# Eleven far taps on SyncE instead of eight, addressed in bytes, in a deformable convolution behind a diffusion stage

## The reference

```
x = x + L0(group_norm(x))     # gates by depthwise 3x3 convolutions, Sobel gradients, 5 diffusion steps
x = x + L1(group_norm(x))     # deformable 3x3 convolution

L1: wi = conv3x3(x, w_offset) + b_offset          # 27 values per pixel: 9 dy, 9 dx, 9 masks
    py, px = base position of the tap + offset    # for each pixel and each of 9 taps
    v00, v01, v10, v11 = the 4 pixels around (py, px), 64 channels each, zero outside the image
    sampled = (bilinear mix of the four) * sigmoid(mask)
    out = sum over taps and channels of sampled * filt
```

## Time and profile before

| | before |
|---|---|
| median of 3 runs | 807.94 us (807.9 to 808.3) |
| the profiled execution, its own time | 803.14 us |
| its span, first to last instruction | 801.3 us |
| granted TensorE clock, mean | 0.904 |
| PE busy | 669.2 us (84%) |
| DVE busy | 539.4 us (67%) |
| POOL busy | 544.0 us (68%) |
| ACT busy | 242.2 us (30%) |
| gathers on POOL | 568 |
| far DMAs on SP | 1024 |

### The profile page before, as it was taken

How to read it: one execution, slowest core, us unless ns; L and a number is a source line. 1 busy time by engine, 2 the same in 40 slices (tenths; PEclk the granted TensorE clock), 3 DMA queues, 4 the chain that set the end, 5 groups by cost and what they waited for, 6 DMA issues and landing times.

```text
span 801.3 us, 15341 instructions
## 1 busy us (share of the span) xinstructions
PE 669.2 (84%) x4616; PEld 589.9 (74%) x4616; DVE 539.4 (67%) x906; ACT 242.2 (30%) x469; POOL 544.0 (68%) x583
## 2 busy tenths in 40 slices
PE   8976888899899988989799987999799987655656
PEld 6865667788788888768689887778778877544545
DVE  5695479778977896578866895778866796322122
ACT  4414421542145213522144313522154213000000
POOL 2000777777777777777777777777777777777774
PEclk9997988999999999999989998999899998555557
DMA  5102333533353433543353435343353335333432
GB/s 167 56 3 55 97 110 109 159 108 115 109 166 109 128 110 112 163 122 109 109 167 114 121 110 167 107 126 108 113 162 114 109 108 167 111 109 108 114 111 72
DMA packets 55146, 92.80 MB, mean 116 GB/s; under 512 B 13384, under 2 KB 35480, under 8 KB 55064
## 3 DMA queue, kind: packets, MB, share of 16 engines
q0 software_dynamic: 27264, 74.49, 31.9%
q1 hardware_dynamic: 27608, 17.20, 7.7%
q10 hardware_dynamic: 192, 0.15, 0.1%
HBM read 79.37 MB, written 12.40 MB: 115 GB/s over the span
## 4 chain that ended last, share of the span: by engine, by line
POOL 57%; issue 20%; PE 12%; DVE 7%; ACT 2%; DMA 1%; POOLq 0%; SPq 0%; DVEq 0%; ACTq 0%
POOL pixels L558 57%; PE banks L1150 9%; PE banks L1153 4%; DVE weighted L903 1%; DMA pixels<-table,index 1%; DVE banks L759 1%; DVE prod L778 0%; DVE prod L798 0%; DVE row_squares L582 0%; ACT coef_T L1051 0%; DVE prod L816 0%; DVE prod L779 0%; ACT sampled_T L1063 0%; DVE banks L760 0%; DMA taps<-taps_in 0%
## 5 line engine op out<-in xcount | busy, mean ns | idle before, releaser
L558 POOL DMA_INDIRECT pixels<-table,index x568 | 538.7, 948 | 247.6 <-issue 172.4
L1153 PE MATMUL banks<-const,weighted 128*128 128x128 f32 x1280 | 194.5, 308 | 62.8 <-DVE weighted L903 49.5
L903 DVE TENSOR_TENSOR weighted<-pixels,banks 128x2304 f32<-128x2304 f32 (+1 forms) x65 | 161.2, 2480 | 115.7 <-DMA pixels<-table,index 111.8
L1153 PEld LDWEIGHTS banks<-const,weighted 128*128 128x128 f32 x1280 | 169.6, 163 | 73.9 <-DVE weighted L903 53.8
L1063 ACT ACTIVATE sampled_T<-banks 128x512 f32<-128x512 f32 (+1 forms) x128 | 55.7, 435 | 335.1 <-PE banks L1153 334.3
L1153 PE MATMUL banks<-const,prod 128*128 128x128 f32 x816 | 109.9, 278 | 19.3 <-DVE prod L778 12.9
L1153 PEld LDWEIGHTS banks<-const,prod 128*128 128x128 f32 x816 | 90.7, 143 | 28.2 <-DVE banks L760 14.1
L1150 PE MATMUL banks<-conv_w,xT 128*128 128x64 f32 (+2 forms) x576 | 97.7, 325 | 0.7 <-ACT banks L1040 0.7
L1150 PEld LDWEIGHTS banks<-conv_w,xT 128*128 128x128 f32 x576 | 91.4, 191 | 7.0 <-ACT banks L1040 1.6
L1150 PE MATMUL banks<-filt,sampled_T 128*128 128x64 f32 x640 | 87.0, 286 | 7.2 <-ACT sampled_T L1063 7.2
L1150 PEld LDWEIGHTS banks<-filt,sampled_T 128*128 128x128 f32 x640 | 81.5, 202 | 13.5 <-ACT sampled_T L1063 11.5
(11 more groups left out here) (144 smaller groups left out, 651.6 us busy)
## 6 DMA issues: line engine op xcount, KB each, us to landing
far_pixels<-table SPq DMA_DIRECT2D x1024, 1.0 KB
pixels<-table,index POOLq DMA_INDIRECT x568, 2.7
table<-xn SPq DMA_DIRECT2D x48, 128.0 KB
table<-xn SPq DMA_DIRECT2D x16, 144.0 KB
x<-x_in SPq DMA_DIRECT2D x30, 64.0 KB, 2.6
out_dram<-x SPq DMA_DIRECT2D x60, 32.0 KB
table<-corner_w SPq DMA_DIRECT2D x16, 70.0 KB
const<-const_in SPq DMA_DIRECT2D x2, 384.0 KB, 3.9
```

What stands on the lines that cost most here:

```text
L558: pool.indirect_dma_start(out=pixels[:, col % NB, k, :], out_offset=None, in_=table[0:(u + 1) * TY * TX, :], in_offset=bass.IndirectOffset ...
L903: return dve.tensor_tensor(weighted[:, col % 2, :, a:b, :].rearrange("p q k c -> p k q c"), entries.rearrange("p k (q c) -> p k q c", c=C) ...
L1153: return pe.matmul(dst, data, moved, start=start, stop=stop, is_transpose=True, skip_group_check=True)
```

## The change

SP fetches the last two taps of the last column of images 2, 4 and 6, and one tap of the others: 11 taps in all instead of 8 (`FAR_TAPS`). POOL gathers three taps fewer. `far_pixels` and the indices (now `far_at`) hold up to two taps. DVE computes the byte address at once (offset added, then times 1024), PE turns one or two columns of indices in its one matmul, and SP reads the table as a flat array of bytes, so that a loaded register is the address as it stands. The fetches of an image are numbered tap by tap: 0 to 127 the first far tap, 128 to 255 the second; the first 32 still come before the output store, and all the rest after it. For the last column of an image with two far taps, DVE's far instruction covers two taps and the other one seven.

```diff
-LAST_TAPS = ((0, 6), (6, 8), (8, K2))
-
-FAR_W, FAR_K = WS - 1, K2 - 1
-FAR_REGS, FAR_FIRST = 16, 32
+LAST_TAPS = ((0, 6), (6, 8))
+
+FAR_TAPS = (1, 1, 2, 1, 2, 1, 2, 1)
+FAR_W, FAR_MOST = WS - 1, max(FAR_TAPS)
+FAR_LOADED, FAR_FIRST = 16, 32
...
-        far_pixels = sb("far_pixels", [P, 2, ENTRY])
-        far_index = sb("far_index", [1, 2, P], u32)
+        far_pixels = sb("far_pixels", [P, 2, FAR_MOST, ENTRY])
+        far_at = sb("far_at", [FAR_MOST, 2, P], u32)
...
+        table_bytes = table.flatten().bitcast(u8)
...
-                for p in range(first, last, FAR_REGS):
-                    sp.load(regs, far_index[0:1, u % 2, p:p + FAR_REGS])
-                    for i in range(FAR_REGS):
-                        sp.dma_start(far_pixels[p + i:p + i + 1, u % 2, :], table[bass.ds(sp.snap(regs[i]), 1), :])\
-                          .then_inc(s_far[u], 16)
+                for n in range(first, last, FAR_LOADED):
+                    tap, p = divmod(n, P)
+                    _, at = nc.values_load_multi_w_load_instructions(
+                        far_at[tap:tap + 1, u % 2, p:p + FAR_LOADED], engines=(mybir.EngineType.SP,), min_val=0,
+                        max_val=(ENTRIES - 1) * 4 * ENTRY, skip_runtime_bounds_check_because="positions are clipped")
+                    for i in range(FAR_LOADED):
+                        sp.dma_start(far_pixels[p + i:p + i + 1, u % 2, tap, :].bitcast(u8),
+                                     table_bytes[bass.ds(at[i], 4 * ENTRY)]).then_inc(s_far[u], 16)
...
-            fetch_far(0, 0, P)
+            fetch_far(0, 0, FAR_TAPS[0] * P)
...
-                        fetch_far(u + 1, FAR_FIRST, P)
+                        fetch_far(u + 1, FAR_FIRST, FAR_TAPS[u + 1] * P)
...
-            return K2 - 1 if col % WS == FAR_W else K2
+            return K2 - (FAR_TAPS[col // WS] if col % WS == FAR_W else 0)
...
-                    dve.wait_ge(s_far[u - 2], 16 * P)
-                dve.tensor_scalar(far_index[0:1, u % 2, :], bank(u, "row")[0:1, 0:P], float(u * TY * TX + LO * TX + LO), None,
-                                  ALU.add).then_inc(s_dve, 1)
+                    dve.wait_ge(s_far[u - 2], 16 * P * FAR_TAPS[u - 2])
+                n = FAR_TAPS[u]
+                dve.tensor_scalar(far_at[0:n, u % 2, :], bank(u, "row")[0:n, 0:P], float(u * TY * TX + LO * TX + LO),
+                                  4.0 * ENTRY, ALU.add, ALU.mult).then_inc(s_dve, 1)
...
-                    dve.wait_ge(s_far[u], 16 * P)
-                    weigh(col, weights, FAR_K, K2, far_pixels[:, u % 2, :].unsqueeze(1))
+                    dve.wait_ge(s_far[u], 16 * P * FAR_TAPS[u])
+                    weigh(col, weights, gathered(col), K2, far_pixels[:, u % 2, 0:FAR_TAPS[u], :])
...
-                at = FAR_W * K2 + FAR_K
-                mm(bank(u, "row")[0:1, 0:P], above[:, at:at + 1], eye, True, True).then_inc(s_full, 1)
+                at, n = (FAR_W + 1) * K2 - FAR_TAPS[u], FAR_TAPS[u]
+                mm(bank(u, "row")[0:n, 0:P], above[:, at:at + n], eye, True, True).then_inc(s_full, 1)
```

More of the change, by code:

```diff
@@ L371, in build_program @@
         s_pixels = [sem(f"pixels_in{j}") for j in range(NB)]
-        s_last = [sem(f"last_pixels_in{j}") for j in range(1, len(LAST_TAPS) - 1)]
+        s_last = [sem(f"last_pixels_in{j}") for j in range(1, len(LAST_TAPS))]
         s_far = [sem(f"far_pixels_in{u}") for u in range(UNITS)]
@@ L382, in build_program @@
         s_a = sem("scalar_step")
+        u8 = mybir.dt.uint8
+        table_bytes = table.flatten().bitcast(u8)
         block = ctx.enter_context(nc.Block())
@@ L490, in write_table @@
                                              k * 2 * C:(k + 1) * 2 * C], pairs).then_inc(s_table, 16)
-            regs = [sp.alloc_register(f"far{i}") for i in range(FAR_REGS)]
             def fetch_far(u, first, last):
@@ L528, in gathered @@
         def gathered(col):
-            return K2 - 1 if col % WS == FAR_W else K2
+            return K2 - (FAR_TAPS[col // WS] if col % WS == FAR_W else 0)
         def arrived(col, k):
             if col == LAST:
-                for i, (a, b) in enumerate(LAST_TAPS[1:-1]):
+                for i, (a, b) in enumerate(LAST_TAPS[1:]):
                     if a <= k < b:
@@ L850, in positions, with far_addresses @@
                 seq(dve.tensor_tensor(ps, ps, lo, ALU.subtract))
-            def far_rows(u):
+            def far_addresses(u):
                 dve.wait_ge(s_full, full(u, "row"))
                 if u >= 2:
-                    dve.wait_ge(s_far[u - 2], 16 * P)
-                dve.tensor_scalar(far_index[0:1, u % 2, :], bank(u, "row")[0:1, 0:P], float(u * TY * TX + LO * TX + LO), None,
-                                  ALU.add).then_inc(s_dve, 1)
+                    dve.wait_ge(s_far[u - 2], 16 * P * FAR_TAPS[u - 2])
+                n = FAR_TAPS[u]
+                dve.tensor_scalar(far_at[0:n, u % 2, :], bank(u, "row")[0:n, 0:P], float(u * TY * TX + LO * TX + LO),
+                                  4.0 * ENTRY, ALU.add, ALU.mult).then_inc(s_dve, 1)
             def corner_weights(u):
@@ L889, in multiply @@
                 weights = weights_now[big % 2][:, j * 4 * K2:(j + 1) * 4 * K2].rearrange("p (k q) -> p k q", q=4)
-                far = w == FAR_W
-                if far:
-                    dve.wait_ge(s_far[u], 16 * P)
-                    weigh(col, weights, FAR_K, K2, far_pixels[:, u % 2, :].unsqueeze(1))
-                for a, b in LAST_TAPS[:-1] if col == LAST else ((0, gathered(col)),):
+                if w == FAR_W:
+                    dve.wait_ge(s_far[u], 16 * P * FAR_TAPS[u])
+                    weigh(col, weights, gathered(col), K2, far_pixels[:, u % 2, 0:FAR_TAPS[u], :])
+                for a, b in LAST_TAPS if col == LAST else ((0, gathered(col)),):
                     if a == 0:
@@ L978, in _ @@
                 elif name == "rowc":
-                    far_rows(n)
+                    far_addresses(n)
                 elif name == "mult":
@@ L1358, in step_own, with far_rows @@
                 ins.then_inc(s_h, 1)
-            def far_row(u):
+            def far_rows(u):
                 pe.wait_ge(s_index, u + 1)
-                at = FAR_W * K2 + FAR_K
-                mm(bank(u, "row")[0:1, 0:P], above[:, at:at + 1], eye, True, True).then_inc(s_full, 1)
+                at, n = (FAR_W + 1) * K2 - FAR_TAPS[u], FAR_TAPS[u]
+                mm(bank(u, "row")[0:n, 0:P], above[:, at:at + n], eye, True, True).then_inc(s_full, 1)
             def turn_back(u):
@@ L1378, in flips @@
                 for k in range(a, b):
-                    for i, taps_of in enumerate(LAST_TAPS[1:-1]):
+                    for i, taps_of in enumerate(LAST_TAPS[1:]):
                         if col == LAST and taps_of[0] == 2 * k:
@@ L1462, in _ @@
                 elif name == "row":
-                    far_row(n)
+                    far_rows(n)
                 elif name == "sum2":
```

## The result

The changed kernel takes 847.66 us, the median of 4 runs (846.2 to 849.2), against 807.92 us before: a ratio of 1.0506, 95% interval 1.0484 to 1.0529. The profiled execution took 847.51 us of its own, against 803.14. From here all differences inside a trace are between these two executions: +44.4 us.

The account below looks back on a forecast made before the run. POOL's gathers, 1.253 us each, were taken to bound the kernel; late tables for images 3, 5 and 7 add 22.6 + 16.7 + 12.6 = +51.9 us, saved gathers included, to the 807.94 us median: 859.8 us, range 828 to 886.

Parts of the forecast that it names:

- POOL bounds, and a gather costs 1.253 us: POOL's row of gathers sets the kernel's time; three gathers fewer take 3.76 us off if POOL never waits.
- The table behind the fetches: In SP's program the next image's table follows all far fetches, so POOL waits 24, 18 and 14 us.
- odd images would wait for nothing: Sign in the trace: no waits for odd images, beside waits named before images 3, 5 and 7.
- The sum of lateness: Late tables from the fetches of images 2, 4 and 6 cost 22.6 + 16.7 + 12.6 = +51.9 us.
- The saving per fetch: On SP, dropping the register instruction and its hand-over saves 0.087 us for each far fetch.
- The base: The +51.9 us was added to the old median, 807.94 us; the profiled execution lay 4.8 us under it.
- At nothing: Effects priced at zero, chiefly DVE waiting for far entries until about 362; up to 13 us without POOL's stop.
- In time after all: Rival: SP's fetches fall below 0.328 us each, no image waits, time 804.2 us; chance 0.09.
- The estimate of 830: Using the skill page's register-load floor of about 600 ns takes 10 us off each SP chain, leaving +22.
- Nothing saved per fetch: Rival: DMAs set SP's pace, a group stays 8.12 us, +118.6 us, time 926.5; chance 0.04.
- The clock on top: Rival: PE idles during the stops and slower stretches follow, adding 15 to 20 us, time 877; chance 0.10.

Follow-up runs that it names:

- e3: The changed kernel, with the next table written after 160 of the 256 fetches in rounds that fetch two taps: 807.43 us, ratio 1.0015.
- e8: The changed kernel with 32 addresses loaded into registers at a time instead of 16: 836.78 us, ratio 1.0365.
- e2: The changed kernel's eleven far taps, but with row numbers and the fused register instruction before each DMA kept: 935.70 us, ratio 1.1595.
- e5: The changed kernel with every table written among the fetches before it, after 80 of 128 or 160 of 256: 838.28 us, ratio 1.0388.
- e6: As e5, but with two far taps in images 1, 3 and 5 instead of 2, 4 and 6: 838.11 us, ratio 1.0383.
- e9: As e3, with the table of image 6 also written early, after 80 of the 128 fetches of image 5: 816.60 us, ratio 1.0113.
- e1: The changed kernel with one far tap in every image, keeping the byte addresses: 805.78 us, ratio 0.9994.
- e12: The changed kernel with two far taps only in images 2 and 5, tables there written after 160 of 256 fetches: 803.02 us, ratio 0.9968.

## Why the prediction was right, and where it was off

**POOL bounds, and a gather costs 1.253 us.** Held. The gathers kept their pace while SP fetched, as the sum had it: 0.946 us and 0.3 us of issue throughout.

**The table behind the fetches.** Held, and shown by e3: the same fetches with the table moved up cost nothing. The three waits stood where I put them, before images 3, 5 and 7, at 20.4, 16.5 and 10.9 us for my 23.9, 17.9 and 13.9. The gathers of even images waited for nothing. (My sign "odd images would wait for nothing" contradicts the three waits named beside it, which stand before odd images; it holds only of the rounds in which SP fetches for an odd image.)

**The sum of lateness**, +51.9 us, against +44.4 in the traces. Term by term for image 2:

| step | predicted | measured |
|---|---|---|
| block of 32 | 11.9 | 11.6 |
| to the next block (store, landing, loads) | 8.6 | 7.7 |
| block of 224 | 92.7 | 91.2 |
| store and table issued | 7.8 | 6.6 |
| table landed | 2.5 | 2.6 |
| whole chain | 123.5 | 119.8 |

No step failed; four were taken 2 to 18% too long, and the errors all point one way. The saving per fetch was 0.093 us, (8.12 - 6.63) / 16, where I had 0.087. Two others I had copied from one round of the old trace, where the store's landing took 3.5 us and a later store 2.4; here they took 1.7 each (the loads of `x` 1.1 us more). Image 6's chain was 114.9 us for 117.1. Image 4's was 120.0 for 120.4. And the chains of images 4 and 6 began about 1 us earlier against POOL than I had assumed: they start from DVE's indices, and those of image 4 came 17.7 us later than before (437.87 against 420.19), where POOL's image 3 had begun 18.5 us later. Against that, the end behind the last gather is 1.2 us longer (11.3 us; the traces of these kernels show 10.1 to 12.9 also where nothing is late).

**The base.** I added the difference to the median. The profiled execution before lay 4.8 us under its median, the one after only 0.2 us under its own, so the medians differ by 39.7 us where the traces differ by 44.4. Of the 12.1 us between 859.8 and 847.66, 7.5 are terms of the sum and 4.7 are this.

**At nothing.** DVE's wait at the last column of image 2 came as described, 12.0 us until 358.1, and was covered: the next column's pixels let DVE start only at 379.18, after 5.3 us more of waiting. I said that without this cover it could cost up to 13 us. e3 removed the cover, the wait at this column grew to 17.8 us, and POOL waited neither for a column (0.3 us in all) nor for the next two tables. So that price was too high: the five column slots are a cover of their own, which I had not counted.

**The rivals.** "In time after all" needed a fetch below 0.328 us with its share of the load. It came to 6.63 / 16 = 0.414. A load kept its 1.228 us for 16 registers in the change, and e8 measured 2.122 for 32. The estimate of 830 had been worked out from the floor of about 600 ns for such a load in the Trainium skill, DMA: Bandwidth & Descriptors, "Latency and other measured facts"; both loads lie well above that floor. "Nothing saved per fetch" is refuted by the 6.63 us of a group, and what it would have cost was run as e2. It measured 935.7, above my 926.5, because SP then falls behind in the one-tap images too, which my sum had excluded. "The clock on top" was right about the clock and wrong about the price. All engines by stretches in the change (columns as in the earlier trace rows):

```profile
346.00:356.00 10.00, 2.64 (x24) 2.40 (x23) 0.07 (x1) 1.32 (x3) 0.00 (x0) 0.78 0.06 17
356.00:366.00 10.00, 3.92 (x10) 2.69 (x11) 7.88 (x16) 0.34 (x2) 0.00 (x0) 0.50 0.52 122
366.00:376.00 10.00, 10.00 (x66) 7.95 (x66) 4.11 (x7) 1.47 (x3) 7.56 (x8) 0.87 0.33 95
```

PE had little to do in the first two and the granted clock fell to 0.50, the 1.2 GHz level. In the stretch in which POOL went on its mean was 0.87. In the whole run POOL waited 0.9 us for weighted columns, so the slower clock didn't reach POOL. (I had read the earlier trace rows as slow stretches behind little PE work. For the first, 0.83, that is not so: PE was busy 10.00 us in the stretch before it, and it was within this stretch that it had less, 7.18.)

## What to carry to other kernels

Where one queue issues both bulk and urgent DMAs, ask not only whether its work fits into the period, but which urgent step stands behind the bulk in its program. Put that step where its input has just come: later, and the bound engine waits; earlier, and the queue idles with the bulk behind it: e5 and e6 lay 31 us above their kernel before. And the bulk itself must have ended before the bound engine's last step, or the end grows (e9, by 12 us). Making each issue cheaper, as the byte addresses do, gained nothing by itself (e1); it gained 2.7 us with two gathers taken from POOL and the tables well placed (e12, 803.02 against 805.72).

## What was unexpected of the hardware

Taking one 44 ns instruction out of SP's stream took 91 to 93 ns out of each fetch, the hand-over with it. A load into registers cost 1.228 us for 16 and 2.122 us for 32, so half as many loads of twice the width save about 0.33 us for each load that is gone. And DVE could be held for 31.5 us at a stretch at one column (e3) without POOL waiting for a column for more than 0.3 us; in e9 it was 44.6 us, at image 6, with 0.9 us of such waits in the whole run.
